# Gated delta net on one core: 16x16 diagonal blocks inverted on VectorE, one block per partition, relayed through DRAM; gram and decay made per head

## The chip, the core and the metric

The program runs on one core of one Trainium2 chip. The core has TensorE (PE in the profile, its weight loads are PEld), VectorE (DVE), ScalarE (ACT), GpSimd (POOL) and SyncE (SP, which issues the DMAs here). Each engine works through its own instructions in order and waits on semaphores that the others count up. The metric is the device time of one execution in microseconds (us), lower is better.

## The reference

Six blocks follow one another over x of shape 2 x 512 x 256: attention and three mixtures of experts, and in between one gated delta net (the fifth of the six in the program; `delta_net` in the kernel). Only the delta net is touched. For each of 16 key heads there are two value heads (GRP = 2) and two batches; the 512 tokens are cut into 8 chunks of 64. What matters is this part, per chunk:

```python
attn = -(jnp.einsum('bhcid,bhcjd->bhcij', k_beta, k) * decay_mask)   # strictly lower, 64 x 64
...
def _correct_row(a, i):
    row = a[..., i, :]
    corr = jnp.einsum('...j,...jk->...k', row, a)
    corr = corr * (jnp.arange(chunk_size) < i)
    return (a.at[..., i, :].set(row + corr), None)
attn, _ = jax.lax.scan(_correct_row, attn, jnp.arange(1, chunk_size))
attn = attn + jnp.eye(chunk_size, dtype=attn.dtype)
value_corrected = jnp.einsum('bhcij,bhcjd->bhcid', attn, v_beta)
...
def chunk_step(state, c):
    ...
    intra = jnp.where(mask_upper1, 0.0, qk * dm_c)
    v_prime = v_c - jnp.einsum('bhld,bhde->bhle', kcd_c, state)
    inter = jnp.einsum('bhld,bhde->bhle', q_c, state) * ge_c[..., None]
    out = inter + jnp.einsum('bhij,bhjd->bhid', intra, v_prime)
    new_state = state * gel_c[..., None] + jnp.einsum('bhld,bhle->bhde', k_c * kd_c, v_prime)
```

The row by row correction is the inverse of a unit triangular 64 x 64 matrix. The chunks of a head depend on one another through the state; the inverses don't.

## The kernel before

`delta_net` is written out fully: `run` goes through one list of steps, and each engine takes from each step what is its own. The list is the order of every engine. One key head (both value heads, both batches) is one body. In a body the chunks go in pairs, and `pair_order(done, build, front, extra)` mixes three pairs: for `done` the state is read and advanced (`read_state`, `new_values`, `update`), for `build` the inverse is made, for `front` the inputs are made (`turn` transposes k and v, `gram` is k times q and k, `decay` multiplies them by the decay, `lower` transposes I plus the gram). The list `extra` holds work of the next head: the projections (`proj` 0 to 11), the convolution taps on DVE (`tap`), the activations (`silu`), the norms, and, in a head's fourth pair, the output: `out_squares`, `out_norm`, `scale_out`, `turn_out`, `project_out`. In the text a head's four calls of `pair_order` are its first to fourth pair.

The inverse is built by doubling. It starts with blocks of size 2 (POOL's `w0` and DVE's step `start`), and each of `LEVELS = 5` levels doubles the size: `z` multiplies the matrix by the inverse so far (L1462), DVE masks that into `zi` (L1818), `e` multiplies again (L1472, and L1476 for the transposed one in all levels but the last), and ACT copies the result into `wt`, after the last level into `winv` (L1560). All are 64 x 64 matmuls in float32, each of which the trace shows as two records.

PSUM banks: `bA` holds even projections, `turn` and `lower` in turn, `bC` odd projections and `gram`. SP issues one load of projection weights `w` (768 KB), one of convolution taps, the decay rows, and one of `wout` per head; it does nothing else.

```python
    yield from both("z", 1)
    yield from through(0, "update")
    yield from both("e", 1)
    yield from extra[2]
```

## Time and profile before

| | |
|---|---|
| median of 3 runs | 3045.74 us (3042.68 to 3046.11) |
| the profiled execution | 3042.04 us, of which the span is 3040.3 us |
| its delta net | from 897 us to some 2560 us of the span |
| one head in the steady part | 106 us |
| TensorE / VectorE / ScalarE / GpSimd busy over the span | 91% / 53% / 42% / 15% |
| mean granted TensorE clock | 0.958 |

The page first gives each engine's busy share, then the span in 40 slices. Views cut to a stretch say what an engine did there and which engine ended its idle time. "issue" is idle time in which no other engine was waited for. A busy PE is one with work in it, and not one at its peak.

### The profile page before, as it was taken

The numbers are of one execution on the slowest core, as the hardware profiler recorded it, in microseconds if no ns is written. First come the engines' busy times: TensorE is split into PE (matmuls) and PEld (weight loads), VectorE is DVE, ScalarE is ACT, GpSimd is POOL, SyncE is SP. The second block draws the span as 40 slices with busy tenths as digits, with TensorE's granted clock in tenths as the row PEclk, the third lists the DMA queues.
The fourth block names the chain that finished last, engine by engine and source line by source line (L and its number), as shares of the span: only waits on it lengthen the run. The fifth ranks groups of instructions, "written<-read, shape, count | busy, mean of one in ns | idle before, by whom it ended". The sixth has DMA issues, their size and how long they took to land. (4 is left out here: it accounts for less than half of the span.)

```text
span 3040.3 us, 79963 instructions
## 1 busy us (share of the span) xinstructions
PE 2766.1 (91%) x33106; PEld 2176.6 (72%) x33106; DVE 1597.8 (53%) x3536; ACT 1285.3 (42%) x2840; POOL 469.5 (15%) x603
## 2 busy tenths in 40 slices
PE   7899888999928999999999999999999999699998
PEld 4433557999815777777777777777777778589997
DVE  4444447666424554555555555555554554476763
ACT  1123212223114555655555565556555555332321
POOL 0011000000001222222222222222222322100000
PEclk9979899999958999999999999999999999899999
DMA  1100011111010000000000000000000000111100
GB/s 43 29 1 1 22 49 56 56 35 48 0 28 23 20 16 12 20 23 5 23 20 16 13 20 23 6 23 20 16 12 20 23 6 6 30 56 55 55 28 14
DMA packets 62021, 73.90 MB, mean 24 GB/s; under 512 B 17152, under 2 KB 51344, under 8 KB 61712
## 3 DMA queue, kind: packets, MB, share of 16 engines
q1 hardware_dynamic: 61712, 69.44, 7.5%
q8 instruction: 235, 3.85, 0.5%
q14 instruction: 74, 0.61, 0.1%
HBM read 68.25 MB, written 1.18 MB: 23 GB/s over the span
## 5 line engine op out<-in xcount | busy, mean ns | idle before, releaser
L433 ACT ACTIVATE g_h<-g_ps,g_b_now 128x512 f32<-128x512 f32 x256 | 175.0, 689 | 338.2 <-PE g_ps L457 332.4
L1472 PE MATMUL dn_ps<-dn_zi,dn_wt 64*64 64x64 f32 x5120 | 253.9, 221 | 56.4 <-DVE dn_zi L1818 55.1
L470 PE MATMUL g_ps<-g_w_high,g_h_low 128*128 128x256 f32 x1024 | 289.8, 283 | 0.0
L470 PE MATMUL g_ps<-g_w_low,g_h_high 128*128 128x256 f32 x1024 | 289.8, 283 | 0.0
L470 PE MATMUL g_ps<-g_w_high,g_h_high 128*128 128x256 f32 x1024 | 289.7, 283 | 0.0
L1818 DVE TENSOR_TENSOR dn_zi<-dn_ps,dn_mz 128x128 f32<-128x128 f32 x640 | 162.8, 286 | 232.4 <-PE dn_ps L1462 229.2
L1472 PEld LDWEIGHTS dn_ps<-dn_zi,dn_wt 64*64 64x64 f32 x5120 | 207.3, 135 | 91.8 <-DVE dn_zi L1818 68.6
L1390 PE MATMUL dn_ps<-xnT,dn_w 128*128 128x512 f32 x512 | 251.4, 616 | 22.7 <-DMA dn_w<-in_W_qkvz_dram 14.9
L1721 POOL TENSOR_TENSOR dn_o<-dn_o,dn_zt 128x256 f32<-128x256 f32 x128 | 107.7, 842 | 963.9 <-DVE dn_o L1845 710.5
L1765 DVE SCALAR_TENSOR_TENSOR dn_cv<-dn_raw,dn_cw,dn_cv 128x1024 f32<-128x1024 f32 x192 | 250.3, 1304 | 2.0
L1560 ACT ACTIVATE dn_wt<-dn_ps 128x256 f32<-128x256 f32 x512 | 187.2, 395 | 100.3 <-PE dn_ps L1476 89.3
L457 PE MATMUL g_ps<-g_x_high,g_w_high 128*128 128x512 f32 x512 | 201.7, 394 | 18.1 <-DVE g_w_low L514 15.6
L1476 PE MATMUL dn_ps<-dn_wt,dn_zi 64*64 64x64 f32 x4096 | 206.7, 219 | 0.0
L1462 PEld LDWEIGHTS dn_ps<-dn_wt,dn_ai 64*64 64x64 f32 x4096 | 145.9, 135 | 82.2 <-issue 48.3
L457 PE MATMUL g_ps<-g_x_low,g_w_high 128*128 128x512 f32 x512 | 201.1, 393 | 0.0
L457 PE MATMUL g_ps<-g_x_high,g_w_low 128*128 128x512 f32 x512 | 200.6, 392 | 0.0
L470 PEld LDWEIGHTS g_ps<-g_w_low,g_h_high 128*128 128x128 f32 x1024 | 196.5, 192 | 0.9
L470 PEld LDWEIGHTS g_ps<-g_w_high,g_h_high 128*128 128x128 f32 x1024 | 196.5, 192 | 0.9
L470 PEld LDWEIGHTS g_ps<-g_w_high,g_h_low 128*128 128x128 f32 x1024 | 196.5, 192 | 0.0
L1462 PE MATMUL dn_ps<-dn_wt,dn_ai 64*64 64x64 f32 x4096 | 176.8, 224 | 21.2 <-ACT dn_wt L1560 20.0
L514 DVE TENSOR_TENSOR g_h_low<-g_h,g_h_high 128x512 fp32r<-128x512 f32 x256 | 177.3, 693 | 8.8
L1838 DVE TENSOR_TENSOR dn_state<-dn_kept,dn_ps 128x512 f32<-128x512 f32 x96 | 66.0, 688 | 208.5 <-PE dn_ps L1518 208.5
(265 smaller groups left out, 5469.7 us busy)
## 6 DMA issues: line engine op xcount, KB each, us to landing
g_w<-in_fc_dram SPq DMA_DIRECT2D x32, 1024.0 KB, 6.5
dn_w<-in_W_qkvz_dram SPq DMA_DIRECT2D x16, 768.0 KB, 4.4
dn_cum_row<-dn_cum_rows SPq DMA_DIRECT2D x32, 256.0 KB, 3.8
dn_wout<-in_W_out_dram SPq DMA_DIRECT2D x16, 256.0 KB, 2.6
f_gate<-in_gateT_dram SPq DMA_DIRECT2D x16, 128.0 KB, 2.1
f_up<-in_upT_dram SPq DMA_DIRECT2D x16, 128.0 KB, 2.3
f_down<-in_downT_dram SPq DMA_DIRECT2D x16, 128.0 KB, 2.4
x_res<-in_x_dram SPq DMA_DIRECT2D x1, 1024.0 KB, 5.2
```

The lines of the kernel that those rows point to most:

```text
L433: nc.scalar.activation(h[:, f % 4], h_b[f % 4], ACT.Gelu, bias=b1_now[u // 2][:, f:f + 1]).then_inc(h_ready, 1)
L457: last = pe.matmul(h_b[f % 4], weights[:, k, f * P:(f + 1) * P], x[:, k, half * BANK:(half + 1) * BANK], start=(k == 0 and n == 0), stop=( ...
L470: last = pe.matmul(y_b[q % 2][:, 0:D], hidden[:, f, q * P:(q + 1) * P], weights[:, f, :], start=(f == 0 and n == 0), stop=(f == NF - 1 and ...
L514: return nc.vector.tensor_tensor(low, whole, high.bitcast(F32), ALU.subtract)
L1390: mm = pe.matmul(to, w[:, k, W_COL[u] * P:(W_COL[u] + 1) * P], m.xnT[:, k, b * T:(b + 1) * T], start=(k == 0), stop=(k == KD - 1))
L1462: mm = pe.matmul(block_of(bD[s], 0, b, h), ai[half(h), s, b, :], inverse[half(h), b, :], start=True, stop=True)
L1472: mm = pe.matmul(block_of(bD[s], 1, b, h), wt[s][half(h), 1, b, :], zi[s][half(h), b, :], start=True, stop=True)
L1476: mm = pe.matmul(block_of(bD[s], 2, b, h), zi[s][half(h), b, :], wt[s][half(h), 1, b, :], start=True, stop=True)
L1560: copy = lambda out, in_, **kw: nc.scalar.activation(out, in_, ACT.Copy, **kw)
L1721: nc.gpsimd.tensor_tensor(o[:, c], o[:, c], zt[f][:, c], ALU.mult).then_inc(s_["oz_r"], 1)
L1765: ins = nc.vector.scalar_tensor_tensor(out=cv[:, u], in0=raw[:, u, :, tap:tap + T], scalar=cw[:, g, tap:tap + 1], in1=cv[:, u], op0=ALU.mu ...
L1818: nc.vector.tensor_tensor(zi[s][:], thirds(bD[s], 0), over_b(mz[l]), ALU.mult).then_inc(s_["Zi_r"], 1)
```

## The change

- The inverse no longer starts at blocks of 2. For each head, the 16 x 16 diagonal blocks of all chunks, batches and value heads (4 x 16 x 2 = 128 of them) are inverted at once on DVE, one block per partition, by 29 chained instructions and a copy of the transpose (`base`). Two levels are left instead of five (`LEVELS = 2`).
- The blocks lie across partitions, and so go through DRAM. `spread` (SP): 8 DMAs store the blocks from `ge`, one DMA loads them with one block per partition. `gather` (SP): after `base` two DMAs store the inverses and their transposes, and 16 DMAs (each 16 partitions x 16 pieces of 64 bytes) load them into `w16` and `w16t`.
- For this, `gram` and `decay` are made for the whole next head ahead of its pairs, two chunks at a time (4 steps per head instead of 8, each of double size), into head-wide `intra` and `ge`. POOL's `w0` and DVE's `start` are gone.
- `pair_order` has 7 places for extra work instead of 8, and the work is laid out anew; `raw` has three slots instead of four; the output of the heads uses `m.xn`, its transpose `oT` two small buffers; `squared` has one buffer. SP follows the same list as the others.

```diff
+BASE = 16
+QUARTERS = C // BASE
+LEVELS = 2
...
 def front_order(j, c):
-    for cc in (c, c + 1):
-        yield from [("turn", j, cc), ("gram", j, cc), ("decay", j, cc)]
-    yield ("lower", j, c)
+    yield from [("turn", j, c), ("turn", j, c + 1), ("unit", j, c), ("unit", j, c + 1), ("lower", j, c)]
...
     yield from both("e", 0)
     yield from extra[1]
+    yield from through(0, "update")
+    yield from ahead(0, "turn")
+    yield from extra[2]
     yield from both("z", 1)
-    yield from through(0, "update")
+    yield from through(1, "read_state")
+    yield from extra[3]
+    yield from through(1, "new_values")
     yield from both("e", 1)
...
+    yield from extra[4]
     yield from through(1, "update")
...
     yield from ahead(1, "turn")
...
+    yield from ahead(0, "unit")
+    yield from ahead(1, "unit")
     yield from extra[5]
...
+    yield from ahead(0, "lower")
     yield from extra[6]
...
+    return [[("rows", j)] + PR(0), PR(1), PR(2) + TP(0, 0), PR(3) + TP(0, 1), TP(0, 2, 3), TP(1, 0, 1), TP(1, 2, 3)]
...
+            SL("k0", "k1"), SL("q") + PR(4), NM(0, 1) + PR(5), NM(2, 3) + TP(2, 0), ONE("norm_roots") + TP(2, 1),
+            ONE("coefs") + ONE("shares") + TP(2, 2), TP(2, 3)])
...
+            GD(0), GD(2), SL("v0") + GD(4), GD(6) + ONE("spread"), PR(6) + PR(7), TP(3, 0, 1), TP(3, 2, 3)])
...
+            SL("v1"), PR(8), PR(9), ONE("base") + ONE("gather") + PR(10), PR(11), [], []])
+        out = [[], [], [], [], [], [("out_squares", j), ("out_norm", j)] + OUT("scale_out", 0, 1),
                OUT("turn_out", 0) + OUT("scale_out", 2, 3) + OUT("turn_out", 1, 2) + OUT("project_out", 0) + OUT("turn_out", 3)
                + OUT("project_out", 1, 2, 3)]
...
+                if name == "proj" and a[0] == 11 and kh + 1 < HK:
+                    load_weights(kh + 1)
...
+                elif name == "spread":
+
+                    wait(sp, "C_e", kh * 4 + 4)
+                    for h in range(GRP):
+                        for t in range(QUARTERS):
+                            rows = slice(h * C + t * BASE, h * C + (t + 1) * BASE)
+                            sp.dma_start(blocks_dram[h, t].rearrange("n r s -> r n s"),
+                                         ge[f][rows, :, t * BASE:(t + 1) * BASE]).then_inc(ge_stored, 16)
+                    sp.wait_ge(ge_stored, (kh + 1) * 16 * GRP * QUARTERS)
+                    wait(sp, "base_r", kh)
+                    sp.dma_start(whole_blocks[:].rearrange("p r s -> p (r s)"),
+                                 blocks_dram.rearrange("h t n r s -> (h t n) (r s)")).then_inc(blocks_loaded, 16)
+                elif name == "gather":
+
+                    wait(sp, "base_r", kh + 1)
+                    for tile, scratch in ((inverse, inverse_dram), (turned, turned_dram)):
+                        sp.dma_start(scratch.rearrange("h t n r s -> (h t n) (r s)"), tile[:].rearrange("p r s -> p (r s)")).then_inc(w16_stored, 16)
+                    sp.wait_ge(w16_stored, (kh + 1) * 32)
...
+                    for tile, scratch in ((w16, inverse_dram), (w16t, turned_dram)):
+                        for h in range(GRP):
+                            for t in range(QUARTERS):
+                                rows = slice(h * C + t * BASE, h * C + (t + 1) * BASE)
+                                sp.dma_start(tile[f][rows, :, t * BASE:(t + 1) * BASE],
+                                             scratch[h, t].rearrange("n r s -> r n s")).then_inc(w16_loaded, 16)
...
                     if l == 0:
                         wait(pe, "AI_r", pair_count(i, j, c) + 1)
-                        wait(pe, "W0_r", chunk(i, j, c) + 1)
+                        pe.wait_ge(w16_loaded, (kh + 1) * 32 * GRP * QUARTERS)
...
+                elif name == "base":
...
+                    dve.wait_ge(blocks_loaded, (kh + 1) * 16)
+                    dve.wait_ge(w16_stored, kh * 32)
+                    then(nc.vector.tensor_tensor(inverse[:], whole_blocks[:], eye16[:], ALU.add))
+                    for t in range(BASE - 2, 0, -1):
+                        n = BASE - 1 - t
+                        products = outer[:, 0:t * n].rearrange("p (r n) -> p r n", r=t)
+                        above = inverse[:, 0:t, t + 1:BASE]
+                        then(nc.vector.tensor_tensor(products, whole_blocks[:, 0:t, t:t + 1].broadcast_to([P, t, n]),
+                                                     inverse[:, t:t + 1, t + 1:BASE].broadcast_to([P, t, n]), ALU.mult))
+                        then(nc.vector.tensor_tensor(above, above, products, ALU.add))
+                    nc.vector.tensor_copy(turned[:].rearrange("p s r -> p r s"), inverse[:]).then_inc(s_["base_r"], 1)
```

How the order moves is shown at two places. The first is where a new head's inverse is begun.

On TensorE before, from the third pair's last `e` and `lower` (L1448, on the last row but two) to the state read (L1486 and L1490) in front of the next head's first `z`:

```order
L1472 MATMUL dn_ps<-dn_zi,dn_wt 64x64 x4
L1476 MATMUL dn_ps<-dn_wt,dn_zi 64x64 x4
L1437 MATMUL dn_ps<-dn_qkk 128x128 x2
L1462 MATMUL dn_ps<-dn_wt,dn_ai 64x64 x8
L1472 MATMUL dn_ps<-dn_zi,dn_wt 64x64 x8
L1448 MATMUL dn_ps<-ident,dn_bi 64x64 x8
L1486 MATMUL dn_ps<-dn_state,dn_qkk 64x128 x4
L1490 MATMUL dn_ps<-dn_state,dn_qkk 64x128 x4
```

On TensorE after, from the state read just ahead of `base` to the next head's first `z` (L1504 with `dn_w`, that is `w16`) and its first projection (L1431). L1438 are projections 10 and 11, L1546 `new_values`, L1513 the last `e`, L1560 and L1564 `update`, L1466 and L1468 `turn`, L1489 `lower`:

```order
L1438 MATMUL dn_ps<-dn_w,xnT 64x128 x16
L1546 MATMUL dn_ps<-dn_wv,dn_winv 64x128 x4
L1513 MATMUL dn_ps<-dn_zi,dn_wt 64x64 x8
...
L1560 MATMUL dn_ps<-dn_vp,dn_kdk 128x128 x4
L1564 MATMUL dn_ps<-dn_vp,dn_intra 64x128 x4
L1466 MATMUL dn_ps<-ident,dn_qkk 128x128 x2
L1468 MATMUL dn_ps<-ident,dn_vv 128x128 x2
L1489 MATMUL dn_ps<-ident,dn_bi 64x64 x8
L1527 MATMUL dn_ps<-dn_state,dn_qkk 64x128 x4
...
L1504 MATMUL dn_ps<-dn_w,dn_ai 64x64 x8
L1431 MATMUL dn_ps<-xnT,dn_w 128x512 x2
```

On SP after, the DMAs of one head from `gather` on (L1389 and L1397, where `dn_w` is `w16`), with the weights of the next head (L1348) behind them:

```order
L1389 DMA dn_inverse_rows<-dn_inverse 128x256
L1389 DMA dn_turned_rows<-dn_turned 128x256
L1397 DMA dn_w<-dn_inverse_rows 16x16x16 x8
L1397 DMA dn_w16t<-dn_turned_rows 16x16x16 x8
L1348 DMA dn_w<-in_W_qkvz_dram 128x2x768
L1357 DMA dn_x<-dn_cum_rows 64x1024 x2
```

Before, the first `z` of a head followed matrices made by POOL and DVE from the head's own gram; now it follows a chain over DVE, SP and DRAM, and two projections, a `new_values`, an `e`, an `update`, a `turn`, a `lower` and a state read stand between.

The second place is the end of a head, on DVE. Before (L1845 is the last chunk's output, L1749 the sum of squares, L1860 the scaling, L1765 and L1762 the taps):

```order
L1762 TENSOR_SCALAR dn_cv<-dn_raw,dn_cw 128x1024
L1845 TENSOR_TENSOR dn_o<-dn_ps,dn_qs 128x256
L1749 TENSOR_REDUCE dn_ssq<-dn_squared 128x4
...
L1765 SCALAR_TENSOR_TENSOR dn_cv<-dn_raw,dn_cw,dn_cv 128x1024
L1749 TENSOR_REDUCE dn_ssq<-dn_squared 128x4
L1852 SCALAR_TENSOR_TENSOR dn_rms<-dn_ssq,dn_cf 128x16
...
L1860 TENSOR_TENSOR dn_o<-dn_o,dn_rms 128x512 x4
```

After (L1898 the last chunk's output, L1788 the sum of squares, L1913 the scaling, L1801 and L1804 the taps):

```order
L1804 SCALAR_TENSOR_TENSOR dn_cv<-dn_raw,dn_cw,dn_cv 128x1024 x3
L1898 TENSOR_TENSOR xn<-dn_ps,dn_qs 128x256
L1788 TENSOR_REDUCE dn_ssq<-dn_squared 128x4
L1801 TENSOR_SCALAR dn_cv<-dn_raw,dn_cw 128x1024
L1804 SCALAR_TENSOR_TENSOR dn_cv<-dn_raw,dn_cw,dn_cv 128x1024
L1788 TENSOR_REDUCE dn_ssq<-dn_squared 128x4
L1905 SCALAR_TENSOR_TENSOR dn_rms<-dn_ssq,dn_cf 128x16
...
L1913 TENSOR_TENSOR xn<-xn,dn_rms 128x512 x2
L1804 SCALAR_TENSOR_TENSOR dn_cv<-dn_raw,dn_cw,dn_cv 128x1024 x2
L1913 TENSOR_TENSOR xn<-xn,dn_rms 128x512 x2
```

Three more taps stand ahead of the last output, another two between it and the sum of squares, and two between the first two and the last two scalings. On TensorE, between the last `update` and the first `turn_out`, there were two levels of the inverse with `turn`, `gram` and a projection before; now there are one `turn` and one `lower`.

## Rows read from the trace of the kernel before

**Rows 1.** Busy by stretch: stretch, length, PE PEld DVE ACT POOL busy, PEclk, DMA.

```profile
1450.00:1556.00 106.00, 98.96 (x1668) 79.02 (x1662) 55.74 (x134) 60.56 (x149) 27.88 (x33) 1.00 0.06 17
1556.00:1665.00 109.00, 101.51 (x1654) 81.53 (x1654) 55.74 (x133) 60.21 (x148) 27.40 (x33) 0.97 0.06 17
```

**Rows 2.** Timeline, TensorE, steady head: start us, us, then what ran.

```profile
1836.35 0.66 PE L1486 MATMUL dn_ps<-dn_state,dn_qkk 128*64 128x128 f32 x8
...
1837.37 0.68 PE L1462 MATMUL dn_ps<-dn_wt,dn_ai 64*64 64x64 f32 x16
1837.99 0.44 PE L1427 MATMUL dn_ps<-ident,dn_qkk 128*128 128x128 f32 x2
...
1838.57 0.65 PE L1505 MATMUL dn_ps<-dn_wv,dn_winv 64*64 64x128 f32 x8
1839.06 0.40 PE L1472 MATMUL dn_ps<-dn_zi,dn_wt 64*64 64x64 f32 x8
...
1840.09 0.71 PE L1437 MATMUL dn_ps<-dn_qkk 128*128 128x128 f32 x4
1840.64 1.88 PE L1390 MATMUL dn_ps<-xnT,dn_w 128*128 128x512 f32 x4
1842.45 0.72 PE L1518 MATMUL dn_ps<-dn_vp,dn_kdk 64*128 64x128 f32 x8
...
1843.58 0.63 PE L1462 MATMUL dn_ps<-dn_wt,dn_ai 64*64 64x64 f32 x16
...
1849.16 0.68 PE L1472 MATMUL dn_ps<-dn_zi,dn_wt 64*64 64x64 f32 x16 [0.16 <-DVE dn_zi L1818]
1849.67 0.63 PE L1448 MATMUL dn_ps<-ident,dn_bi 64*64 64x64 f32 x16
1850.24 1.98 PE L1390 MATMUL dn_ps<-xnT,dn_w 128*128 128x512 f32 x4
```

**Rows 3.** Timeline, VectorE: chained instructions of 256 columns, and one of 16.

```profile
885.60 0.42 DVE L1094 TENSOR_TENSOR dng_e<-dng_e,dng_um 128x256 f32<-128x256 f32 x1
886.06 0.42 DVE L1095 TENSOR_TENSOR dng_u<-dng_u,dng_e 128x256 f32<-128x256 f32 x1
...
1923.33 0.17 DVE L1852 SCALAR_TENSOR_TENSOR dn_rms<-dn_ssq,dn_cf 128x16 f32<-128x16 f32 x1
```

**Rows 4.** Timeline, SP: start us, us of the issue; x4 are four in a row.

```profile
846.55 7.53 SPq L1018 DMA_DIRECT2D dng_dt<-in_dt_bias_dram  x1
893.74 1.77 SPq L1023 DMA_DIRECT2D dn_cum_rows<-dng_by_row  x4
...
1674.05 0.35 SPq L1348 DMA_DIRECT2D dn_cw<-in_conv_dram  x1
```

**Rows 5.** Page, DMA issues: name, engine, count, KB each, us from issue to landing.

```profile
dn_w<-in_W_qkvz_dram SPq DMA_DIRECT2D x16, 768.0 KB, 4.4
...
f_gate<-in_gateT_dram SPq DMA_DIRECT2D x16, 128.0 KB, 2.1
```

**Rows 6.** DMA view, same columns: the load in 64-byte pieces, stores to DRAM.

```profile
dn_cw<-in_conv_dram SPq DMA_DIRECT2D x16, 8.0 KB, 1.6
...
dn_cum_rows<-dng_by_row SPq DMA_DIRECT2D x4, 32.0 KB, 1.6
```

**Rows 7.** Groups by line, one steady head: taps, copies after `turn`; busy us, mean ns.

```profile
L1765 DVE SCALAR_TENSOR_TENSOR dn_cv<-dn_raw,dn_cw,dn_cv 128x1024 f32<-128x1024 f32 x12 | 15.6, 1303 | 0.1
...
L1560 ACT ACTIVATE dn_kdk<-dn_ps,dn_cf 128x128 f32<-128x128 f32 x16 | 5.0, 364 | 8.0 <-PE dn_ps L1429 7.7 <-issue 0.3
```

**Rows 8.** Timeline, all engines, end of a head: last output to first `turn_out`.

```profile
1917.03 0.43 DVE L1845 TENSOR_TENSOR dn_o<-dn_ps,dn_qs 128x256 f32<-128x256 f32 x1 [4.09 <-PE dn_ps L1522]
...
1921.95 0.62 ACT L1679 ACTIVATE dn_squared<-dn_o 128x512 f32<-128x512 f32 x1
...
1925.35 0.52 PE L1534 MATMUL dn_ps<-ident,dn_o 128*128 128x128 f32 x3
```

**Rows 9.** Busy by stretch (columns as Rows 1), behind the norms of a head.

```profile
1136.00:1139.40 3.40, 3.40 (x56) 3.38 (x58) 2.89 (x5) 0.58 (x2) 0.00 (x0) 0.50 0.02 5
```

More of the change, by code:

```diff
@@ L1128, in prepare_order @@
         yield from [("proj", j, 2 * u, "A"), ("proj", j, 2 * u + 1, "C")] + [("tap", j, u, n) for n in range(CONV)]
-    yield from [("silu", j, u) for u in ("k0", "k1", "q")] + [("proj", j, m, "AC"[m % 2]) for m in range(8, 12)]
-    yield from [("norms", j, n) for n in range(4)] + [("norm_roots", j), ("coefs", j), ("shares", j)] + [("silu", j, u) for u in ("v0", "v1")]
+    yield from [("silu", j, u) for u in ("k0", "k1", "q")]
+    yield from [("norms", j, n) for n in range(4)] + [("norm_roots", j), ("coefs", j), ("shares", j)]
+    for c in range(0, NCH, 2):
+        yield from [("gram", j, c), ("decay", j, c)]
+    yield ("spread", j)
+    yield from [("silu", j, u) for u in ("v0", "v1")] + [("proj", j, m, "AC"[m % 2]) for m in range(8, 12)]
+    yield from [("base", j), ("gather", j)]
 def front_order(j, c):
-    for cc in (c, c + 1):
-        yield from [("turn", j, cc), ("gram", j, cc), ("decay", j, cc)]
-    yield ("lower", j, c)
+    yield from [("turn", j, c), ("turn", j, c + 1), ("unit", j, c), ("unit", j, c + 1), ("lower", j, c)]
 def pair_order(done, build, front, extra=[[]] * 8):
@@ L1152, in pair_order @@
     yield from through(0, "read_state")
-    yield from both("start")
     yield from both("z", 0)
@@ L1196, in body_order @@
         prep = not (last and j == 1)
-        early = early_order(j + 2) if not last else [[]] * 8
+        early = early_order(j + 2) if not last else [[]] * 7
         q = j + 1
-        PR = lambda n, bank: [("proj", q, n, bank)] if prep else []
+        PR = lambda n: [("proj", q, n, "AC"[n % 2])] if prep else []
         TP = lambda u, *ns: [("tap", q, u, n) for n in ns] if prep else []
@@ L1365, in _ @@
+            load_weights(0)
+            load_taps(0)
+            load_rows(0)
+            load_out(0)
+            run(sp, step)
         @block.tensor
@@ L1385, in step @@
                     else:
-                        wait(pe, "C_e", i * 16 + so_far["gram"])
+                        wait(pe, "C_e", i * 8 + so_far["gram"])
                     to = bA if where == "A" else bC
@@ L1433, in step @@
                     f = j % 2
-                    wait(pe, "C_e", chunk(i, j, c))
+                    if c == 0:
+                        wait(pe, "sl", kh * 5 + 3)
+                    wait(pe, "C_e", pair_count(i, j, c))
                     wait(pe, "ev", i * 24 + so_far["proj"])
-                    for b in range(B):
-                        mm = pe.matmul(bC[:, part(b)], k_twice(f, b, c), q_and_k(f, b, c), start=True, stop=True)
+                    for n in range(2 * B):
+                        mm = pe.matmul(bC[:, part(n)], k_twice(f, n % B, c + n // B), q_and_k(f, n % B, c + n // B), start=True, stop=True)
                     mm.then_inc(s_["C_r"], 1)
@@ L1458, in step @@
                         wait(pe, "WT_r", level(i, j, c, l - 1) + 1)
-                    inverse = wt[s][:, 0] if l else w0[s]
+                    inverse_of = wt[s][:, 0] if l else of_chunk(w16[f], c)
                     for b in range(B):
                         for h in range(GRP):
-                            mm = pe.matmul(block_of(bD[s], 0, b, h), ai[half(h), s, b, :], inverse[half(h), b, :], start=True, stop=True)
+                            mm = pe.matmul(block_of(bD[s], 0, b, h), ai[half(h), s, b, :], inverse_of[half(h), b, :], start=True, stop=True)
                     mm.then_inc(s_["Z_r"], 1)
@@ L1466, in step @@
                     s = c % 2
-                    if l == 0:
-                        wait(pe, "T2_r", chunk(i, j, c) + 1)
+                    turned_of = wt[s][:, 1] if l else of_chunk(w16t[j % 2], c)
                     wait(pe, "Zi_r", level(i, j, c, l) + 1)
@@ L1521, in step @@
                         for h in range(GRP):
-                            mm = pe.matmul(bF[half(h), part(2 + b)], intra[c % 4][half(h), b, :], vp[half(h), b, :],
+                            mm = pe.matmul(bF[half(h), part(2 + b)], of_chunk(intra[f], c)[half(h), b, :], vp[half(h), b, :],
                                            start=True, stop=True)
@@ L1723, in _ @@
             start_counts(pool, pool_sems)
+            for tile in w16 + w16t:
+                nc.gpsimd.memset(tile[:], 0.0).then_inc(s_["z16"], 1)
             nc.gpsimd.memset(raw[:, :, :, 0:CONV - 1], 0.0)
```

187 lines of the change are left out of this document (86 added, 101 removed).

## The prediction

> **What bounds the kernel now.** I read the engine table first, then the delta net cut into heads, then TensorE's timeline inside one head, and last what every idle gap of it waits for. A steady head takes 106 us, in which TensorE is busy for 98.96 us and idle for 7.0; DVE works for 55.7, ACT for 60.6 [rows 1]. So TensorE's own list is the path, and the other engines matter where TensorE waits for them. There are no long gaps: the work of three pairs and of the next head is mixed so that nearly each product finds other matmuls beside it. The order is fixed, so the question is both how much matmul time goes and what cover it took along.
>
> **What goes.** The costs of the steps are distances between starts on TensorE [rows 2]. `z` of a pair of chunks is 0.62 us (1837.37 to 1837.99), `e` with its transpose 1.03 (1839.06 to 1840.09), the last `e` 0.51 (1849.16 to 1849.67). Three levels of `z` and full `e` go: 3 x 1.65 = 4.95 us per pair, 19.8 us per head. That leaves 99.0 - 19.8 = 79.2 us of TensorE work in a head. The other steps keep their cost: state read 1.02, `turn` 0.58, `new_values` 0.49, `gram` 0.55 per chunk (double steps, half as many), projection 1.81, `update` 1.13, `lower` 0.57 [rows 2]. POOL's `w0` and DVE's `start` go, and DVE loses 24 masks per head; none of them is late next to a TensorE that is busy 93% of the time, and I take nothing for them.
>
> **What comes, first place: the relay.** `base` is 30 instructions on DVE, each waiting for the one before. A chained 256-column one has a pitch of 0.46 us at 0.42 busy, one of 16 columns is busy 0.17 [rows 3], so 0.04 lies between. The first one is 0.46. The 28 inner ones have 13 to 56 columns, 40 on average; on the line between the two rows that is 0.20, with the gap 0.24 each, 6.7 in all. The copy is at most another 0.4. Sum 7.5 us. DVE does nothing else in that time; the next state waits behind it.
>
> Then SP: two stores of 128 KB. Four stores were issued in 1.77 us, 0.44 each [rows 4]; landing takes 1.6 us for 32 KB to DRAM and 2.1 for a 128 KB load [rows 6, 5], I take 2.1. So 0.1 + 0.44 + 2.1 = 2.6, and with the wake-up of SP 2.7. Then 16 loads in 64-byte pieces, 256 pieces each. The nearest row for the pieces is the taps' load, 128 of them in 1.6 us; I take 1.9 for twice as many. The nearest one for the issue is 0.44, with 0.35 at the lower end. 15 x 0.47 + 1.9 = 9.0, of which 0.03 each is my allowance for three-dimensional patterns. The relay is 2.7 + 9.0 = 11.7 us, `base` and relay 19.2.
>
> The first `z` of the new head waits for all of it. What TensorE has meanwhile, counted from the state read ahead of `base` (which starts 0.3 us later, when DVE has made the two `wv`): two projections 3.7, `new_values` 0.49, last `e` 0.51, `update` 1.13, `turn` 0.58, `lower` 0.57, state read 1.02: 8.0 us. `lower` and that state read are themselves late behind `base` on DVE and POOL, which is inside the same wait. **Wait at `z`: 19.2 + 0.3 - 8.0 = 11.5 us** per head. By the bounds: issues of 0.35, landings of 1.6 and `base` of 6.5 make it 7.7. At the other end stands the load of `dng_dt`, 1024 pieces of 4 bytes behind three more such loads, for which SP was held 7.53 us [rows 4]: a full queue stretches the issues. If 64-byte pieces filled it so, 4096 of them would hold SP for up to 30 us per head.
>
> Behind the 16 loads SP issues the next head's weights (before, they were loaded a quarter of a head ahead of use). They land 0.47 + 4.4 us [rows 5] after the last of the 16 is issued, `z` starts 1.9 after it and takes 0.6, and the next instruction is projection 0: **2.3 us** more of waiting. The first half of the relay, `spread` (9 DMAs, some 9 us by the same rows), has about 13 us of TensorE work from the last `decay` to `base`, and costs nothing unless the rows are off by half.
>
> The Trainium skill, DMA: Bandwidth & Descriptors, section Anatomy of one DMA, puts most of a fixed 2 us per DMA down to the receipt of the write. With that for both hops my 2.1 + 1.9 would be 4.0 as well, so batching the 16 loads would save issues but not the two receipts; no row here splits a landing into its parts.
>
> **Second place: the end of a head.** The last chunk's output goes DVE, POOL, ACT, DVE, ACT, DVE, and then TensorE turns it. Before, 8.3 us lay between the output and `turn_out` [rows 8], with two levels of the inverse, a projection and a `turn` to fill them. From the start of the squares to `turn_out` it is 3.4 us at least (1921.95 to 1925.35). Now DVE has a sum of squares and two taps (0.6 + 0.75 + 1.3) between output and last sum: 0.5 + 2.65 from `update` to the sum, then 0.73 + 0.17 + 0.25 + 0.4 + 0.8 to the end of the first scaling, 5.5 us. `turn` and `lower` cover 1.15: wait 4.3. Then two more taps of 1.3 [rows 7] stand ahead of the third scaling: 0.65 + 2.6 + 0.75 = 4.0 against two `turn_out` of 0.55: wait 2.9. Together **7.2 us** that the old order did not have.
>
> **Third, bank A.** `turn` writes it, and ACT's four copies of 0.36 (pitch 0.3) free it 1.2 us later [rows 7]. Now `lower` comes directly behind `turn` in every pair, and projection 2 directly behind another: in the first two pairs and there I count 3 x 1.2 = **3.6 us** (in the third the relay hides it, in the fourth the output). In the third pair four taps stand ahead of the `wv` that `new_values` needs: 2.6 us. Against these, the old 7.0 us of small waits: those at levels that are gone go too, I keep 3.0.
>
> Sum of a head at full clock: 79.2 + 11.5 + 2.3 + 7.2 + 3.6 + 2.6 + 3.0 = **109.4 us**, against 106.
>
> **The clock.** Where TensorE was granted half its clock (1.2 GHz) for 6.8 us the head took 109 instead of 106 [rows 1]; in the stretch behind the norms, when it had run one-column matmuls for some 4 us, it was at 0.50 [rows 9]. After a wait of 11 us with little work I expect that level at least once per head: +3 us. The Trainium skill, TensorE: Matmul & The Clock Gate, section HAM oscillation, says the same of kernels that wait for data in each iteration; the trace of before has no wait of that length in its steady part, so no row here tests it. If the clock held, a head would be at 109.4. With the term it is 112.4 per head, +6.4. Fifteen heads prepare a next one: +96 us. The first head has its relay nearly bare (some +15), the last has no relay and three pairs with less work (-8). 3042 + 96 + 7 = 3145 for the profiled execution; the median of the runs lies 3.7 above the profiled one: **3149 us**.
>
> **The rivals.** (a) The savings win. The relay is at its lower end (wait 7.7), the clock stays up, and the queue on DVE drains early enough that the output chain costs its bare length, 3.4 + 1.2 - 1.15 = 3.5: 79.2 + 7.7 + 2.3 + 3.5 + the old 7.0 = 99.7, -6.3 per head, -95 in all with the ends at nothing: about 2950. It speaks for it that 19.8 us are certain and every wait is my count; against it, that even this lower end eats two thirds of the saving. It decides where all waits of a head stay under 26.8 us. (b) The queue fills. SP's issues stretch from 0.47 towards what the 4-byte pieces showed; 12 us more per head give 3149 + 180 = about 3330. The taps' load in 64-byte pieces speaks against it. (c) The two sides cancel, within 0.2%: waits of 26 to 28 us per head. (d) The relay and the output wait are as forecast but the clock holds: 109.4 per head, 3149 - 45 = about 3100; that is inside my range and slower.
>
> **How the numbers follow.** Forecast with (d) 0.64, (a) 0.24, (b) 0.07, (c) 0.05. A measurement of this kernel can tell some 0.2% from no change. Faster 0.24, within 0.2% 0.05, slower 0.71. The range reaches over half of (a) and half of (b): 2970 to 3250. The likeliest case alone: 3085 to 3210.
>
> **What would show it.** In the profile after: heads of 109 to 115 us; in each one wait of 10 to 13 us on TensorE at L1504 for the DMA into `w16`; a second one of 2 to 3 us at L1431 for the weights; 4 and 3 us at L1576 for DVE's scaling; 16 issues at L1397 in 7 to 8 us; `base` 7 to 8 us; PEclk 0.5 behind the long wait. It is wrong if L1504 hardly waits (the relay is faster than its issues), if the waits at the end of a head are under 3 us, or if TensorE's busy time per head is not 79 at full clock.

## The result, and the profile after

The changed kernel takes **3189.8 us** (median of 4 runs, 3184.36 to 3195.3) against 3044.8: ratio 1.0477, 95% interval 1.0458 to 1.0496. The forecast was 3149 us in a range of 2970 to 3250, slower.

I cut the same seven heads out of each trace, from one load of the convolution taps to the seventh after it, as stretch, length, then PE, PEld, DVE, ACT and POOL busy with counts, PEclk, DMA share and GB/s. Before:

```profile
1353.18:2097.25 744.07, 694.34 (x11594) 555.08 (x11596) 389.67 (x932) 422.67 (x1030) 193.66 (x224) 1.00 0.06 17
```

After:

```profile
1390.34:2202.67 812.33, 635.92 (x7564) 481.57 (x7562) 399.29 (x862) 359.65 (x854) 179.31 (x168) 0.83 0.10 22
```

A head went from 106.3 to 116.0 us. TensorE ran a third fewer matmul records (11594 to 7564), yet its busy time fell from 99.2 to 90.8 us only, because its granted clock fell from 1.00 to 0.83; its idle time rose from 7.1 to 25.2 us. That is 9.7 us for each of the 15 heads that prepare a next one, 146 us, and the median moved by 145.

The relay, on TensorE's timeline (start, us, what ran, in brackets the idle time before it and its releaser); L1438 is the projection beside `base`, L1504 with `dn_w` the `z` that needs the relay:

```profile
1980.34 1.92 PE L1438 MATMUL dn_ps<-dn_w,xnT 128*64 128x128 f32 x32
...
1986.63 0.38 PE L1468 MATMUL dn_ps<-ident,dn_vv 128*128 128x128 f32 x2
1990.68 1.12 PE L1489 MATMUL dn_ps<-ident,dn_bi 64*64 64x64 f32 x16 [3.67 <-POOL dn_bi L1746]
1991.73 1.12 PE L1527 MATMUL dn_ps<-dn_state,dn_qkk 128*64 128x128 f32 x8
1992.64 1.07 PE L1531 MATMUL dn_ps<-dn_state,dn_qkk 128*64 128x128 f32 x8
1999.42 1.12 PE L1504 MATMUL dn_ps<-dn_w,dn_ai 64*64 64x64 f32 x16 [5.71 <-issue]
2002.36 3.78 PE L1431 MATMUL dn_ps<-xnT,dn_w 128*128 128x512 f32 x4 [1.83 <-DMA dn_w<-in_W_qkvz_dram]
```

VectorE in that time, the first and last instructions of `base` and the state that stood behind them:

```profile
1980.64 0.42 DVE L1856 TENSOR_TENSOR dn_inverse<-dn_whole_blocks,dn_eye 128x256 f32<-128x256 f32 x1
1981.09 0.18 DVE L1861 TENSOR_TENSOR dn_outer<-dn_whole_blocks,dn_inverse 128x14 f32<-128x14 f32 x1
...
1987.69 0.38 DVE L1864 COPY dn_turned<-dn_inverse 128x256 f32<-128x256 f32 x1
1987.91 0.67 DVE L1891 TENSOR_TENSOR dn_state<-dn_kept,dn_ps 128x512 f32<-128x512 f32 x1
```

SP, the issues of the relay and the weights behind it:

```profile
1988.10 0.32 SPq L1389 DMA_DIRECT2D dn_inverse_rows<-dn_inverse  x1
1988.46 0.43 SPq L1389 DMA_DIRECT2D dn_turned_rows<-dn_turned  x1
1990.29 3.75 SPq L1397 DMA_DIRECT2D dn_w<-dn_inverse_rows  x8
1994.08 3.88 SPq L1397 DMA_DIRECT2D dn_w16t<-dn_turned_rows  x8
1998.01 0.45 SPq L1348 DMA_DIRECT2D dn_w<-in_W_qkvz_dram  x1
```

One serial path: `base` 7.4 us, stores until the first load 2.2, sixteen loads issued in 7.7 (0.48 each, as against the 0.35 and 0.44 of [rows 4]), `z` 1.5 us after the last issue. From `base` to `z` it is 18.8 us. TensorE idles 3.67 + 5.71 us of them, and at 1990.68 it comes back at half clock: the state read of 1.02 [rows 2] takes 2.0, and projection 0 takes 3.78 against the 1.88 of the same four records before.

The end of the same head, TensorE from the last `turn` on (L1576 is `turn_out`, L1587 `project_out`), which answers to [rows 8]:

```profile
2020.45 0.38 PE L1468 MATMUL dn_ps<-ident,dn_vv 128*128 128x128 f32 x2
2023.95 1.12 PE L1489 MATMUL dn_ps<-ident,dn_bi 64*64 64x64 f32 x16 [3.12 <-POOL dn_bi L1746]
2025.71 1.94 PE L1576 MATMUL dn_ps<-ident,xn 128*128 128x128 f32 x8 [0.64 <-DVE xn L1913]
...
2029.43 1.09 PE L1576 MATMUL dn_ps<-ident,xn 128*128 128x128 f32 x4 [1.77 <-DVE xn L1913]
2030.31 3.55 PE L1587 MATMUL dn_ps<-dn_wout,dn_oT 128*128 128x256 f32 x8
```

The page's groups (count, busy us, mean ns, then idle time just before, and what ended most of it) show where the waits stand in all 16 heads:

```profile
L1431 PE MATMUL dn_ps<-xnT,dn_w 128*128 128x512 f32 x512 | 298.9, 721 | 60.1 <-DMA dn_w<-in_W_qkvz_dram 41.0
...
L1489 PE MATMUL dn_ps<-ident,dn_bi 64*64 64x64 f32 x1024 | 58.0, 270 | 179.1 <-POOL dn_bi L1746 174.2
```

The largest of all is 179 us at `lower`. In the head shown it is 3.67 (relay), 3.12 (output), 1.23 and 3.10 us (first and second pair). The prediction had the first two inside its waits for the relay and the output, and 1.2 each, for bank A, in the other two.

### The profile page after: what moved, and what is told of

It is laid out like the page before. It is cut to its first block and busy times, and to the rows that moved or that the text cites. A ratio compares the mean times of both kernels' runs of the same rounds, so it can differ in the third digit from the quotient of the medians.

```text
span 3188.6 us, 60191 instructions
## 1 busy us (share of the span) xinstructions
PE 2620.2 (82%) x23890; PEld 1999.5 (63%) x23890; DVE 1616.2 (51%) x3376; ACT 1142.0 (36%) x2442; POOL 438.4 (14%) x479
## 5 line engine op out<-in xcount | busy, mean ns | idle before, releaser
L1431 PE MATMUL dn_ps<-xnT,dn_w 128*128 128x512 f32 x512 | 298.9, 721 | 60.1 <-DMA dn_w<-in_W_qkvz_dram 41.0
L1804 DVE SCALAR_TENSOR_TENSOR dn_cv<-dn_raw,dn_cw,dn_cv 128x1024 f32<-128x1024 f32 x192 | 282.3, 1470 | 5.3
L1758 POOL TENSOR_TENSOR xn<-xn,dn_zt 128x256 f32<-128x256 f32 x128 | 99.3, 776 | 1198.5 <-DVE xn L1898 856.9
L1871 DVE TENSOR_TENSOR dn_zi<-dn_ps,dn_mz 128x128 f32<-128x128 f32 x256 | 66.5, 286 | 312.4 <-PE dn_ps L1504 308.1
L1489 PE MATMUL dn_ps<-ident,dn_bi 64*64 64x64 f32 x1024 | 58.0, 270 | 179.1 <-POOL dn_bi L1746 174.2
L1431 PEld LDWEIGHTS dn_ps<-xnT,dn_w 128*128 128x128 f32 x512 | 103.7, 221 | 161.6 <-issue 128.2
L1489 PEld LDWEIGHTS dn_ps<-ident,dn_bi 64*64 64x64 f32 x1024 | 49.1, 176 | 192.9 <-issue 154.8
L1602 ACT ACTIVATE dn_raw<-dn_ps 128x512 f32<-128x512 f32 x128 | 76.2, 595 | 205.1 <-PE dn_ps L1431 205.1
L513 DVE CAST g_h_high<-g_h 128x512 fp32r<-128x512 f32 x256 | 109.0, 426 | 78.8 <-ACT g_h L435 77.8
L565 DVE SCALAR_TENSOR_TENSOR x_res<-g_ps,g_w,x_res 128x256 f32<-128x256 f32 x128 | 61.8, 483 | 171.9 <-PE g_ps L472 171.9
```

Of the source, the lines that this page charges most:

```text
L513: nc.vector.tensor_copy(high, whole).then_inc(high_made, 1)
L1431: mm = pe.matmul(to, w[:, k, W_COL[u] * P:(W_COL[u] + 1) * P], m.xnT[:, k, b * T:(b + 1) * T], start=(k == 0), stop=(k == KD - 1))
L1489: mm = pe.matmul(block_of(bA, n, b, h), bi[n][half(h), b, :], eye_of(h), start=True, stop=True)
L1602: copy = lambda out, in_, **kw: nc.scalar.activation(out, in_, ACT.Copy, **kw)
L1758: nc.gpsimd.tensor_tensor(o[:, c], o[:, c], zt[f][:, c], ALU.mult).then_inc(s_["oz_r"], 1)
L1804: ins = nc.vector.scalar_tensor_tensor(out=cv[:, u], in0=raw[:, u % 3, :, tap:tap + T], scalar=cw[:, g, tap:tap + 1], in1=cv[:, u], op0=AL ...
```

## The experiments

All are edits of the changed kernel. From the same view over the same seven heads, divided by seven (idle is length less TensorE's busy time; the work that nobody reads, filler in the table, counts as busy):

| kernel | time, us | head | PE busy | idle | PEclk |
|---|---|---|---|---|---|
| before | 3044.8 | 106.3 | 99.2 | 7.1 | 1.00 |
| after | 3189.8 | 116.0 | 90.8 | 25.2 | 0.83 |
| without gather | 3024.0 | 105.8 | 87.8 | 18.0 | 0.89 |
| without base's chain | 3102.9 | 110.3 | 90.1 | 20.2 | 0.86 |
| base early | 3053.9 | 106.3 | 88.6 | 17.7 | 0.88 |
| POOL's bi first | 3192.1 | 116.0 | 88.3 | 27.8 | 0.87 |
| taps out of the output | 3114.7 | 110.2 | 85.9 | 24.3 | 0.88 |
| filler, 5 products | 3195.4 | 116.5 | 94.4 | 22.1 | 0.87 |
| filler, 12 products | 3160.6 | 113.9 | 97.4 | 16.5 | 0.91 |
| first combination | 2987.0 | 103.4 | 84.8 | 18.7 | 0.93 |
| second combination | 2942.1 | 100.4 | 84.4 | 16.0 | 0.93 |
| third combination | 2869.1 | 94.6 | 81.5 | 13.1 | 0.97 |

### Is the relay the path?

```diff
 elif name == "gather":
-    wait(sp, "base_r", kh + 1)
-    (2 stores, waits, 16 loads)
+    pass
...
-dve.wait_ge(w16_stored, kh * 32)
...
-pe.wait_ge(w16_loaded, (kh + 1) * 32 * GRP * QUARTERS)
+wait(pe, "z16", 4)
```

> Leaves out the second half of the relay: SP neither stores the inverted blocks nor loads them with its 16 DMAs, and the first z of a head waits for none of that; the start matrices w16 and w16t stay zero, so the inverse and all that follows from it is not the reference's. base still runs on VectorE. Theory 1 (the relay is the path, and the half clock behind it is its consequence): the idle 5.7 us at L1504 and the 1.8 us of L1431 waiting for the weights go, and some 5 of the 12.7 us per head that the lower clock costs come back: 12.5 us per head, 15 heads, 3190 - 190 = about 3000 us, mean granted clock up from 0.82-0.84 to about 0.88 in a head. Rival A (the clock is held down by the other waits of a head all the same): only the idle time goes, 7.5 us per head: about 3077 us, clock below 0.85. Rival B (base's own 7.4 us on VectorE is what TensorE waits for, and the states and POOL's bi behind it): the wait moves from L1504 to L1489, L1527 and L1546, under 3 us per head are won: 3150 us or more.

Measured 3024.0 us, 166 less: 11.1 per head, of which 7.2 are idle time and 3.0 TensorE's own work at a better clock (seven heads alone: 10.2; the rest lies outside them). The idle 3.67 at `lower` stays, and behind it the half clock, so the gain falls short of theory 1 by 24 us. Rival A is 53 us off on the other side, and rival B falls.

```diff
-for t in range(BASE - 2, 0, -1):
-    ... (28 chained instructions)
```

> Leaves out the 28 inner instructions of base: the inverse of a block is the block plus the identity, which is not the reference's. The sum with the identity, the copy of the transpose and the whole relay stay. Theory 1 (base is the first 7.4 us of one serial path base, stores, 16 loads, z): z comes 6.6 us earlier, and of the 9.4 us of idle time ahead of it 6.6 go, with 2 to 4 us of clock: 3030 to 3070 us. Rival F (base lies beside TensorE work that is needed anyway, and only the 11.7 us of DMAs are the path, as leaving them out gave 166 us): under 3 us per head, 3145 us or more.

Measured 3102.9 us, 87 less, 5.8 per head: between the two, nearer to theory 1. TensorE's timeline where `base` would have been (columns as above):

```profile
1944.35 0.68 PE L1489 MATMUL dn_ps<-ident,dn_bi 64*64 64x64 f32 x16 [1.67 <-POOL dn_bi L1746]
...
1949.47 1.12 PE L1504 MATMUL dn_ps<-dn_w,dn_ai 64*64 64x64 f32 x16 [2.53 <-issue]
...
1952.48 3.78 PE L1431 MATMUL dn_ps<-xnT,dn_w 128*128 128x512 f32 x4 [1.89 <-DMA dn_w<-in_W_qkvz_dram]
```

Of 3.67 + 5.71 us, 1.67 + 2.53 are left: 5.2 gone for 6.6 taken off VectorE. Both halves, `base` and DMAs, are on one path. But here little clock came back (0.86): 1.9 us of waiting for the weights still follow, and projection 0 still takes 3.78.

```diff
-SL("v1"), PR(8), PR(9), ONE("base") + ONE("gather") + PR(10), PR(11), [], []])
+SL("v1") + ONE("base") + ONE("gather"), PR(8), PR(9), PR(10), PR(11), [], []])
```

> The computation is whole; only the order changes: base and gather stand in the third pair's first extra place instead of its fourth, so that two more projections, an e, an update, a turn and a z (about 7.5 us of TensorE work) lie between them and the z that needs them. Theory 1 (relay on the path): the idle time in front of the first z falls from 9.4 us (5.7 at L1504, 3.7 at L1489) to 3 us or less, the weights come in time or nearly so, and part of the clock's 12.7 us comes back: 9 to 12 us per head, 3020 to 3055 us. Rival A (other waits hold the clock down): 6 to 7 us per head, about 3090 us. Rival B (base itself is the cost): base now stands in front of zi and of the state of a pair whose TensorE work depends on them, so the wait only moves: within 15 us of 3190. A further way to fail: the blocks' load has landed some 13 us ahead of base, and the early place uses up about 10 of them.

Measured 3053.9 us, 136 less with nothing left out: 9.1 per head, the low end of theory 1's gain, from the place of two words in a list. Ratio to the kernel before 1.003 (1.0004 to 1.0056). The wait at `z` is all but gone, the one for the weights is not, other than theory 1 had it, and behind it projection 0 still runs at half clock:

```profile
1914.56 0.68 PE L1489 MATMUL dn_ps<-ident,dn_bi 64*64 64x64 f32 x16 [1.67 <-POOL dn_bi L1746]
...
1917.33 0.68 PE L1504 MATMUL dn_ps<-dn_w,dn_ai 64*64 64x64 f32 x16 [1.07 <-issue]
1920.34 3.78 PE L1431 MATMUL dn_ps<-xnT,dn_w 128*128 128x512 f32 x4 [2.32 <-DMA dn_w<-in_W_qkvz_dram]
```

### The waits at lower

```diff
+    yield from ahead(0, "unit")
+    yield from ahead(1, "unit")
     yield from through(1, "update")
     yield from ahead(1, "turn")
-    yield from ahead(0, "unit")
-    yield from ahead(1, "unit")
```

> The computation is whole; only POOL's order changes: its two bi (I plus the gram, which lower transposes) stand ahead of the product of the chunk's output with z, and not behind it. That product waits for VectorE's last output of the pair. Theory 2 (the 3.1, 3.1 and 3.7 us that TensorE idles at L1489 per head are due to POOL's order, and not to bank A or VectorE): these 9.9 us fall to the 1.2 us that ACT's copies out of bank A take: some 1.2 x 3 remain, 6 us per head at least and more with the clock, 15 heads: 3100 us or less. Rival A (the wait has a second cause just behind, ACT's copies or the relay, which starts no earlier): the wait at L1489 is renamed to ACT dn_vt or moves to L1504 in the fourth pair; 2 x 1.9 = 4 us per head, about 3130 us. Rival C (what TensorE saves there it waits for VectorE's state or the relay anyway): within 15 us of 3190.

Measured 3192.1 us: nothing, rival C. The waits at `lower` did fall to 1.23 us each, and the next one stood right behind each of them, in this kernel's timeline ahead of `z`, `turn_out` and the third pair's `new_values`:

```profile
2004.14 1.12 PE L1504 MATMUL dn_ps<-dn_w,dn_ai 64*64 64x64 f32 x16 [9.42 <-issue]
...
2031.16 1.94 PE L1576 MATMUL dn_ps<-ident,xn 128*128 128x128 f32 x8 [2.90 <-DVE xn L1913]
...
2090.91 0.92 PE L1546 MATMUL dn_ps<-dn_wv,dn_winv 64*64 64x128 f32 x8 [2.90 <-DVE dn_wv L1879]
```

The 2.90 at `new_values` is the prediction's 2.6 us for the four taps in a row, which the profile after does not show: it lay under the wait at `lower`. The releaser that a profile names is the last of several, and here the runner-up was close behind in all three places. Not even the clock helped: TensorE's own work fell by 2.6 us per head (0.87 instead of 0.83), and its idle time rose by the same 2.6.

### The end of a head

```diff
-[("out_squares", j), ("out_norm", j)] + OUT("scale_out", 0, 1),
-OUT("turn_out", 0) + OUT("scale_out", 2, 3) + OUT("turn_out", 1, 2) + OUT("project_out", 0) + OUT("turn_out", 3)
+[("out_squares", j), ("out_norm", j)] + OUT("scale_out", 0, 1, 2, 3),
+OUT("turn_out", 0, 1, 2) + TPE(1, 0, 1) + OUT("project_out", 0) + OUT("turn_out", 3) + OUT("project_out", 1)
...
```

> The computation is whole; only the order at the end of a head changes: the two taps between the last output and its sum of squares, and the two between the second and the third scaling, stand behind all four scalings, two of them between turn_out and project_out. Theory 1 (the output's chain over five engines is bare on TensorE, and taps stretch it): the idle 3.1 + 0.6 and 1.8 us per head at L1576 fall to about 2.2, with some clock back, 4 us per head: about 3130 us. Rival D (the taps are needed soon enough by the next head's activations and masks, so that the wait comes back at its z, its silu or its norms): within 15 us of 3190. Rival E (the chain of squares, root and reciprocal is as long bare, POOL's product above all): the wait at L1576 stays at 3 us, about 3165 us.

Measured 3114.7 us, 75 less, 5.0 per head by the medians: more than theory 1 asked for. Over the seven heads it is 5.8, and only 0.9 of that is idle time; 4.9 us are TensorE's own work, at 0.88 instead of 0.83. The same place in this kernel's timeline:

```profile
1978.70 0.68 PE L1491 MATMUL dn_ps<-ident,dn_bi 64*64 64x64 f32 x16 [1.70 <-POOL dn_bi L1748]
...
1981.38 3.13 PE L1578 MATMUL dn_ps<-ident,xn 128*128 128x128 f32 x12 [2.00 <-DVE xn L1915]
1984.31 2.85 PE L1589 MATMUL dn_ps<-dn_wout,dn_oT 128*128 128x256 f32 x8
```

Two waits of 1.7 and 2.0 in place of 3.12, 0.64 and 1.77, and `lower` runs at full clock (0.68 against 1.12 for the same 16 records). `turn_out` does not: the granted clock is 0.50 over 1981.38 to 1984.31, and `project_out` gets full clock within its first eight records (2.85 us for them against 3.55). Most of the gain lies further on, around the norms. First after, then this kernel, the same projection:

```profile
2048.14 3.78 PE L1431 MATMUL dn_ps<-xnT,dn_w 128*128 128x512 f32 x4
...
2001.09 1.98 PE L1433 MATMUL dn_ps<-xnT,dn_w 128*128 128x512 f32 x4
```

In all seven heads here it takes 1.98 us; after, it takes 3.4 to 3.8 in six of the seven. From the norms to the next `lower` TensorE's work is 11.4 us per head against 13.7, and from the output's `lower` to its last `project_out` 13.1 against 14.1. The clock is where the gain is; that the shorter waits brought it is argued from their order in time, as this edit changed several things at once.

### The clock by itself

```diff
+if c == 0 and kh > 0:                      # ahead of lower (2) and of z (3, then 7)
+    wait(pe, "WT_r", level(i, j, 0, 0))
+    for n in range(3):
+        pe.matmul(bD[0], m.xnT[:, 0, 0:P], m.xnT[:, 0, 0:T], start=True, stop=True)
```

> The computation is whole and its order that of the changed kernel. TensorE gets work that nobody reads, in the one wait of each head for the relay: two products of 128x512 ahead of lower and three ahead of z, 0.94 us each at full clock (4.7 us in all) and 1.88 at half (9.4 us), as long as the idle time there. Theory 1 (the half clock of some 16 us behind the relay's wait is due to TensorE's idleness in it, and is the term that the prediction had too small): the clock stays up behind z, 3 to 6 us per head come back though nothing was taken away: 3100 to 3145 us. Rival G (the low clock has to do with load or with the other half clock stretches of a head, not with this wait): the clock in a head stays at 0.82 to 0.84, and the added work costs 0 to 3 us per head: 3190 to 3235 us.

Measured 3195.4 us, 6 more: no verdict. The time is rival G's, the clock (0.87) is above the 0.82 to 0.84 that it asked for, though the added products at full clock raise that mean by themselves. Full clock was kept to `z` (0.68 us), but 4.26 us of idle were left ahead of it and 2.36 behind it, and projection 0 had half clock again:

```profile
2004.73 0.68 PE L1512 MATMUL dn_ps<-dn_w,dn_ai 64*64 64x64 f32 x16 [4.26 <-issue]
...
2007.77 3.78 PE L1431 MATMUL dn_ps<-xnT,dn_w 128*128 128x512 f32 x4 [2.36 <-DMA dn_w<-in_W_qkvz_dram]
```

So the second one fills both, with 7 products ahead of `z` and 3 ahead of projection 0.

> As the kernel with work that nobody reads in the relay's wait, which left 4.3 us idle ahead of z and 2.4 ahead of projection 0, behind which the clock fell all the same: now seven products of 128x512 ahead of z (6.6 us at full clock) and three in bank A ahead of projection 0 (2.8 us), besides the two ahead of lower. The computation is whole. Theory 1 (the half clock behind the relay follows TensorE's idleness there): full clock at z and at projections 0 and 1, whose 3.78 us for two products become 1.98; the half clock stretch up to the output goes, mean clock in a head 0.90 or more; 3 to 5 us per head come back, 3115 to 3150 us. Rival G (the clock falls somewhere in a head anyway, and the stretch only moves): projections 0 to 3 or the stretch behind them run at half clock as before, 3180 to 3240 us. Rival I (the clock stays up, but what TensorE saves it waits for others, VectorE's output chain above all): clock 0.90 or more and yet 3170 us or more, with longer idle times at L1576 and L1489.

```profile
1984.45 0.68 PE L1515 MATMUL dn_ps<-dn_w,dn_ai 64*64 64x64 f32 x16 [0.81 <-issue]
1985.06 2.84 PE L1430 MATMUL dn_ps<-xnT 128*128 128x512 f32 x6
1987.74 1.88 PE L1434 MATMUL dn_ps<-xnT,dn_w 128*128 128x512 f32 x4
```

Measured 3160.6 us, 29 less than after, though work was added and none removed. Projection 0 takes 1.88 us instead of 3.78 (1.9 to 2.0 in all seven heads, against 3.5 to 3.8), the clock in a head is 0.91. That shows the cause of this stretch: the half clock behind the relay comes of TensorE's idleness there. The size is below my 3 to 5 us: twelve products of 0.94 are 11.3 us, so TensorE's own work fell from 90.8 to 86.1, by 4.7 us per head (somewhat more, as the added products ran partly at half clock in three of the seven heads), and the head by 2.2. The rest was waited away further on (rival I in part): at the end of a head it still waits 3.13, 1.08 and 1.78 us.

### Together

The first combination has `base` early, POOL's `bi` first, the output without taps, `turn` of the second chunk ahead of `update`, and `z` waiting for the first 8 loads only, `e` for the other 8:

```diff
+    yield from ahead(1, "turn")
     yield from through(1, "update")
-    yield from ahead(1, "turn")
...
-pe.wait_ge(w16_loaded, (kh + 1) * 32 * GRP * QUARTERS)
+pe.wait_ge(w16_loaded, (kh + 1) * 16 * GRP * QUARTERS)
```

> The computation is whole. Together: base and gather in the third pair's first extra place, POOL's bi ahead of its product, the output's chain free of taps, turn of a pair's second chunk ahead of update instead of behind it (so that ACT's four copies out of bank A lie beside update), and z waits for the first 8 of the 16 loads only, e for the other 8. Theory 1 (the waits are separate terms of one sum on TensorE): 9.1 us per head from the early base and 5.0 from the tail, as each gave alone, 3 x 1.2 at bank A, 1 to 2 from the split, 17 to 20 us per head: 2890 to 2940 us, under the kernel before. Rival H (they overlap: behind one removed wait VectorE is late with the next, as POOL's order showed, which gave nothing alone): 2970 to 3040 us.

Measured 2987.0 us, ratio to the kernel before 0.9806 (0.9789 to 0.9824), 203 less than after. The two parts measured alone give 136 + 75 = 211: they do not quite add up, and what was new in it, POOL's `bi` first included, gave nothing on top, rival H. VectorE is late with `wv` (3.42 us ahead of `new_values`), behind four taps in a row.

The second combination, by its main lines (projections 6 and 7, in the first pair's list, are left out here; `gather_turned` issues the second 8 loads):

```diff
-            GD(0), GD(2), SL("v0") + GD(4), GD(6) + ONE("spread"), PR(6) + PR(7), TP(3, 0, 1), TP(3, 2, 3)])
+            GD(0) + TP(3, 0), GD(2), GD(4) + TP(3, 1), GD(6) + ONE("spread") + TP(3, 2), SL("v0") + TP(3, 3), PR(8), []])
-            SL("v1") + ONE("base") + ONE("gather"), PR(8), PR(9), PR(10), PR(11), [], []])
+            SL("v1") + ONE("base") + ONE("gather"), PR(9), PR(10), PR(11) + ONE("gather_turned"), [], [], []])
```

> The computation is whole. As the combination beside it, and moreover: projections 6 and 7 lie in the first pair and 8 in the second, so that the last four taps go one by one between VectorE's other work in the second pair instead of four in a row ahead of the third pair's wv; the second 8 loads of the relay are issued behind the next head's weights. Theory 1: the 2.9 us that TensorE idles at L1546 behind the taps and the 2.3 us for the weights go, and 1 us comes in front of z for the missing projection: 2 to 4 us per head less than the combination beside it, 2830 to 2900 us. Rival H (the weights' issue waits for projection 11 and so holds back the second 8 loads; fewer projections are left to lie beside the relay): the same as the combination beside it or up to 30 us more.

Measured 2942.1 us (0.9663, 0.9646 to 0.9681), 45 less: 3.0 per head, the gain that theory 1 asked for, from a higher start, so that its range in us was missed by 42. Rival H is out.

The third combination, again by its main lines:

```diff
-PR = lambda n: [("proj", j, n, "AC"[n % 2])]
+PR = lambda n: [("proj", j, n, "CACC"[n])]
...
+GD(0) + TP(3, 0), GD(2), GD(4) + TP(3, 1), GD(6) + ONE("spread") + TP(3, 2), TP(3, 3), PB(8, "C"), SL("v0")])
```

> The computation is whole. As the second combination, and moreover: projections change banks so that none goes into bank A directly behind turn (1.3 us of idle twice per head, 0.7 once); the activation of v0 with its table load of 1.28 us stands behind turn's copies instead of ahead of them (2.75 us at projection 8); the squares of the output stand behind turn's copies on ScalarE; projection 3 lies beside the output's chain (2.64 us at turn_out). Theory 1 (each idle gap on TensorE is a term of its own): of 13 us of idle per head 6 to 8 go, with 1 to 2 us of clock: 2942 - 15 x 7 to 9 = 2810 to 2840 us. Rival H (they overlap, the relay is next): under half of it, 2880 to 2920 us.

Measured **2869.1 us**, ratio to the kernel before **0.942** (0.9391 to 0.9449), 73 less than the one before it, 4.9 per head, between the two theories; over the seven heads it is 5.8, half of it idle time and half clock. Seven heads of it:

```profile
1317.62:1979.86 662.24, 570.24 (x7573) 433.26 (x7574) 387.19 (x861) 356.44 (x855) 159.98 (x168) 0.97 0.12 27
```

94.6 us a head, with the same arithmetic as the changed kernel. It is not free of waits: ahead of the output's `lower` 3.5 to 3.7 us are left in each of the seven heads, and in the one at 1789.02 us the granted clock behind them is 0.50. Whether the kernel before would gain from such an order too was not tried; with 7.1 us of idle per head and the clock at 1.00 it has less to gain.

## Why the prediction was right, and where its sum was off

The sum of a head was 79.2 of work + 30.2 of waits + 3 for the clock = 112.4; it measured 116.0 = 79.2 + 25.2 + 11.6. The direction and its mechanism, TensorE waiting for the relay and for the output, were right. That the total came as near as 41 us is in part luck: the waits were 5.0 per head too high, the clock 8.6 too low. Of the signs listed, the issues (7.7), `base` (7.4), the weights (1.83, just under 2) and the half clock behind the long wait came as written or nearly so; the head (116.0 for 109 to 115), the single wait of 10 to 13 at L1504 (5.71, with 3.67 at `lower` ahead of it) and the 4 and 3 us at L1576 (0.64 and 1.77, with 3.12 at `lower` ahead) did not.

- **Work, 79.2 at full clock.** Right. In the third combination TensorE is busy for 81.5 us at 0.97, which leaves no more than 2.3 us for all that I did not count. The split of 90.8 into 79.2 and 11.6 rests on this 79.2.
- **`base`, 7.5 us.** 7.4 measured: 0.17 to 0.22 busy for the inner ones (14 to 56 columns, where I had written 13), with pitches of 0.21 to 0.25.
- **Relay, 11.7 us, `z` at 19.2.** 11.4 and 18.8. The stores landed a little sooner than my 2.1 (1.7 and 1.8 in the DMA view), the loads in 1.8 for my 1.9, and the issues took 0.48 for the 0.47 that I had allowed. The rival of a full queue is out for 64-byte pieces; what held SP for the 7.53 us of [rows 4] no run here tells. The section that I drew on there, Anatomy of one DMA in the Trainium skill's DMA: Bandwidth & Descriptors, gives its 2 us for DMAs issued by GpSimd, and these are issued by SP.
- **Wait at `z`, 11.5.** 9.4 idle, in two pieces. Some 1.4 us of the rest is that the work between them ran at half clock (3.0 us for 1.6): slow work inside a wait shortens the wait. Weights 1.8 for 2.3.
- **End of a head, 7.2.** 0.64 and 1.77 are named as such, and 3.12 of the wait in front of it is named after POOL; 5.5 in all. The chain is what I counted, yet its price was more than its idle time, by the clock.
- **Bank A and `wv`, 3.6 + 2.6.** Two of the three places at bank A came as counted, 1.23 at the first pair's `lower` in the head shown (1.8 for POOL in the others) and 1.28 at projection 2. The third has the wrong mechanism, as have the waits at `lower` in the relay and the output: `lower` waited 3.1 to 3.7 us in three pairs of four for POOL's `bi`, which stood behind POOL's product of the output. I named POOL only in passing. As reordering it alone gave nothing, the sum was hardly hurt: other waits of nearly the same length lay behind it, the taps among them. The 2.6 for `wv` lay under the second pair's 3.10, and was counted as well.
- **Small waits, 3.0.** 2.1 in the head shown.
- **Clock, 3 us.** This is the term that was mis-sized: 11.6. I had taken one half clock stretch of 6.8 us as in [rows 1]. The profile after has five in the head shown: behind the relay's wait to the end of projection 0, behind the output's wait, twice around the norms, and behind the wait at `lower` in the second pair. My own list had waits of 11.5, 4.3 and 2.9 us, and I put a price for the clock on the first alone. The fillers test the first of the five stretches: in the run that fills its waits, 4.7 of the 11.6 us are gone. The others were not isolated. And 11.6 is what the slow work took, not what the head would gain without it: 4.7 less gave 2.2 in the run with 12 products, 2.6 less gave nothing in the one with `bi` first.

The Trainium skill, TensorE: Matmul & The Clock Gate, section HAM oscillation, says that a kernel which waits for data in each iteration starts every iteration cold. The trace agrees: projection 0, behind the relay's wait, takes 3.5 to 3.8 us in each of the seven heads of after, against 1.88 before, and the run with 12 products without a use, which got 29 us back, bears the cause out.

The gain that the change was to bring, 19.8 us per head, thus came off TensorE's list and went into waits (18.1 more) and clock (11.6). It is to be had in part: with the steps in an order that cuts the waits to 13.1 us, the head is 11.7 us shorter than before.

## What to carry to other kernels

When an edit takes matmul work away and adds waits, give each wait a second price, that of the slow matmuls behind it: here 25.2 us of idle per head came with 11.6 us of clock, and taps moved out of the output's chain gave 4.9 us of clock for 0.9 of idle. It is an upper bound, as slow work that lies inside another wait costs nothing. A serial chain over another engine and DRAM is cheap where it is started early enough; here moving two steps from the fourth place of a list to the first was worth 136 us. And where a wait is named after one engine, look for the runner-up before giving a price to its removal: an edit that takes away the named cause alone can give nothing (`bi` first). Whether it is of use once the others are gone, no run here shows.
